# Attention between two feed-forward phases: value matmuls at other steps of a head pair, their eviction on ScalarE, one batch's output by single token tiles

## The chip, the core and the metric

The kernel runs on 1 core of one Trainium2 chip. The metric is the device time of one launch in microseconds (us). The engines are TensorE (PE; its weight loads are a row of their own, PEld), VectorE (DVE), ScalarE (ACT), GpSimd (POOL) and SyncE (SP), which issues the DMAs. PSUM has 8 banks of 512 float32 per partition.

## What is computed

Two batches of 1024 tokens with 128 channels go through a feed-forward block (itself an attention with 16 small heads and a mixture of expert projections), then a causal attention with one shared key/value head of 64, then the feed-forward block again. The middle part is the one that matters here:

```python
q = (x @ Wq).reshape(b, n, 16, 64).transpose(0, 2, 1, 3) * scale
kv = concatenate([null_kv, x @ Wkv], axis=1)        # keys and values are the same
sim = einsum('bhid,bjd->bhij', q, kv)               # causal mask
attn = softmax(sim)
out = einsum('bhij,bjd->bhid', attn, kv)
x = x + out.reshape(b, n, 16 * 64) @ Wout
```

x is the layer-normed input inside the attention; each block adds to the stream.

## The kernel before

The attention goes by head pairs: 8 pairs of 2 heads in each of 2 batches, 16 pairs in all. A pair has 16 steps (`STEPS`): query tiles 0 to 3 of head 0, the same of head 1 (the lower half of the tokens), then query tiles 4 to 7 of either head (the upper half). A step works on 128 queries with 129, 257, ... 1024 keys, so steps 3, 7, 11 and 15 are the longest of their fours.

The steps run through a pipeline with its order written out per engine. In step t TensorE makes the scores of tile t (`a_score_tile`, L1387 and L1389, the mask added by L1394) into one of two pairs of banks, by turns; it waits for the exponential of tile t-2 first. Then come the transposes of tile t-4 (`a_transposes`, L1407; `A_LAG` is 4), in two halves of 64 queries in two banks. DVE reduces the maximum (L1021), copies the second half of the transposes of tile t-4 (L1046) and makes the reciprocal of the sum of tile t-2 (L1040). ACT copies the first half (L727) and makes the exponential of tile t (L720). GpSimd multiplies the probabilities by the reciprocal (L637), ahead of the transposes. Every engine takes its instructions in order.

Into this go, on TensorE:

- the value matmuls `a_values` (L1423), in parts of two key tiles, all into bank 7 (`PV_BANK`). The lower half has two parts, the upper half four. They run in the next pair: lower in its steps 0 and 1 (`V0_STEPS`), upper in its steps 4, 5, 8, 12 (`V1_STEPS`; 4, 5, 8, 9 in the first pair of the second batch). At the end of a half DVE evicts the bank (`o_evac`, L1056)
- the next pair's queries in two halves (`queries`, L1369) in steps 3 and 6, evicted in part by ACT (L705) and in part by DVE (L1015, `query_1`) one step later; then SP copies them across partitions (`build_q_s`)
- in the first pair of the second batch, steps 13 and 14, the output of the first batch (`outputs`, L1433 and L1434): each time four token tiles of nine matmuls, in bank 7, and DVE adds them to x (`add_out`, L1063)

Transposes and queries share three banks (`T_BANKS`), taken by turns in a list of 34 takes a pair (`TAKES`). 34 is not a multiple of 3: the last take of a pair, the second half of the transposes of tile 11 in step 15, is put into a bank by hand, and `taken_before` finds which eviction a take has to wait for. DVE's order in step t is maximum(t), copy(t-4), reciprocal(t-2), eviction of a half of the values, `query_1`, evicted upper half, add. ACT's is copy(t-4), query, exponential(t).

Of the kernel before, what the change touches and what calls it, by code (L numbers as in the profile page):

```python
# [7 lines left out]
ALU = mybir.AluOpType  # L8
# [8 lines left out]
def build(nc, x_in, a_wq, a_wkv, a_null, a_wout, f_wq, f_bq, f_wk, f_bk, f_wv, f_bv,  # L17
# [22 lines left out]
    with ExitStack() as ctx:  # L40
# [157 lines left out]
        ay_done = sem("ay_done")  # L198
        x_loaded = [sem(f"x_loaded_{b}") for b in range(B)]
# [62 lines left out]
        for t in range(NS):  # L262
            TAKES += [("T", (t - A_LAG) % NS, half) for half in range(2)]
            if t in Q_STEPS:
                TAKES.append(("Q", Q_STEPS.index(t), 0))
# [3 lines left out]
        def taken_before(take, pair):  # L269

            i = TAKES.index(take)
            for back in range(1, 2 * len(TAKES)):
                turn, j = pair + (i - back) // len(TAKES), (i - back) % len(TAKES)
                kind, n, half = TAKES[j]
                if TAKE_BANK[TAKES[j]] != TAKE_BANK[take]:
                    continue
                if kind == "T":
                    tile = NS * turn + n - (NS if n >= NS - A_LAG else 0)
                    if tile >= 0:
                        return kind, half, tile  # L280
                elif 0 <= turn < B * PAIRS - 1:
                    return kind, n, turn + 1
            return None
# [368 lines left out]
        def _(act):  # L652
# [46 lines left out]
            def query_0(pg, par, h):  # L699

                if h == 0 and (not isinstance(pg, int) or pg >= 2):
                    act.wait_ge(a_scores, NS * pg - NS)
                act.wait_ge(proj_done, 2 * pg + h + 1)
                bank = TAKE_BANK["Q", h, 0] if pg else (PV_BANK, Q_BANK)[h]
                nc.scalar.activation(q_s[0:AD, par, 0, h * HALF:(h + 1) * HALF], ps[0:AD, bank, :], ACT.Copy,  # L705
                                     scale=A_SCALE).then_inc(q0_ready, 1)
# [16 lines left out]
            def a_evac(pg, t):  # L723
                qh, hh, qt = STEPS[t]
                m = qt + 1
                act.wait_ge(tr_done[0], NS * pg + t + 1)
                nc.scalar.activation(probs_T[qh][:, hh, 0:m, (qt % 4) * P:(qt % 4) * P + ROWS],  # L727
                                     ps[:, TAKE_BANK["T", t, 0], 0:m * ROWS].rearrange("p (k q) -> p k q", q=ROWS), ACT.Copy).then_inc(evac_act, 1)

            def attention():  # L730
# [13 lines left out]
                def body(b, pl, first, last):  # L744
                    for k in range(2):
                        pg = b * PAIRS + pl + k
                        for t in range(NS):
                            if first:
                                second_batch(k, t)
                            if t >= A_LAG:  # L750
                                a_evac(pg, t - A_LAG)
                            elif not (first and k == 0):
                                a_evac(pg - 1, NS + t - A_LAG)
                            if t - 1 in Q_STEPS and not (last and k == 1):
                                query_0(pg + 1, (k + 1) % 2, Q_STEPS.index(t - 1))
                            a_exps(pg, t)
                for b in range(B):
                    body(b, 0, b == 0, False)
                    for i in range(1, PAIRS // 2 - 1):
                        body(b, i * 2, False, False)  # L760
                    body(b, PAIRS - 2, False, b == B - 1)
                for t in range(NS - A_LAG, NS):
                    a_evac(B * PAIRS - 1, t)

                norm_std(2 * B, 0)
                norm_T(2 * B, 0, 5)
# [56 lines left out]
        def _(dve):  # L823
# [185 lines left out]
            def query_1(pg, par, h):  # L1009
# [4 lines left out]
                bank = TAKE_BANK["Q", h, 0] if pg else (PV_BANK, Q_BANK)[h]  # L1014
# [27 lines left out]
            def a_evac(pg, t):  # L1042
# [4 lines left out]
                                      ps[:, TAKE_BANK["T", t, 1], 0:m * ROWS].rearrange("p (k q) -> p k q", q=ROWS)).then_inc(evac_dve, 1)  # L1047
# [6 lines left out]
            def o_evac(pg, pl, qh):  # L1054
                dve.wait_ge(apv_done, 2 * pg + qh + 1)
                nc.vector.tensor_scalar(o_T[:, bass.ds(pl, 1), qh * HALF:(qh + 1) * HALF].rearrange("p a b -> p (a b)"),  # L1056
                                        ps[:, PV_BANK, :], 1.0, None, ALU.mult).then_inc(pv_bank_free, 1)

            def add_out(b, g, bank):

                dve.wait_ge(ay_done, 2 * b + g + 1)
# [3 lines left out]
            def attention():  # L1065
                dve.sem_inc(pv_bank_free, 2)

                def second_batch(pair, t):
# [10 lines left out]
                    if (pair, t) == (1, 15):  # L1079
                        null_scores_in(1, PV_BANK)  # L1080

                def body(b, pl, switch, first, last):
                    for k in range(2):
                        pg = b * PAIRS + pl + k
                        turn = switch and k == 0
                        before = (b - 1, PAIRS - 1) if turn else (b, pl + k - 1)
                        for t in range(NS):
                            if first:
                                second_batch(k, t)
                            a_maximum(pg, t)  # L1090
                            if t >= A_LAG:
                                a_evac(pg, t - A_LAG)
                            elif not (first and k == 0):
                                a_evac(pg - 1, NS + t - A_LAG)
                            if t >= 2:
                                a_recip(pg, t - 2)
                            elif not (first and k == 0):
                                a_recip(pg - 1, NS + t - 2)
                            if t - 1 == V0_STEPS[-1] and not (first and k == 0):
                                o_evac(pg - 1, before[1], 0)  # L1100
                            if t - 1 in Q_STEPS and not (last and k == 1):
                                query_1(pg + 1, (k + 1) % 2, Q_STEPS.index(t - 1))
                            if t - 1 == (V1_TURN if turn else V1_STEPS)[-1] and not (first and k == 0):
                                o_evac(pg - 1, before[1], 1)
                            if turn and t - 1 in Y_STEPS:
                                add_out(b - 1, Y_STEPS.index(t - 1), PV_BANK)
                for b in range(B):
                    body(b, 0, b > 0, b == 0, False)
                    for i in range(1, PAIRS // 2 - 1):
                        body(b, i * 2, False, False, False)  # L1110
                    body(b, PAIRS - 2, False, False, b == B - 1)
                pg = B * PAIRS - 1
                for t in range(NS - 2, NS):
                    a_recip(pg, t)
                o_evac(pg, PAIRS - 1, 0)
                for t in range(NS - A_LAG, NS):
                    a_evac(pg, t)

                norm(2 * B, 0)
                o_evac(pg, PAIRS - 1, 1)  # L1120
# [64 lines left out]
        def _(pe):  # L1185
# [162 lines left out]
            def wait_taken(take, pair):  # L1348

                before = taken_before(take, pair)  # L1350
                if before is not None:
                    kind, n, g = before
                    if kind == "Q":
                        pe.wait_ge(q0_ready, 2 * g + n + 1)
                        pe.wait_ge(q1_ready, 2 * g + n + 1)
                    else:
                        pe.wait_ge(evac_dve if n else evac_act, g + 1)

            def queries(pg, b, h):

                if pg:
                    wait_taken(("Q", h, 0), pg - 1)
                    bank = TAKE_BANK["Q", h, 0]
# [34 lines left out]
            def a_transposes(pg, t):  # L1398
# [3 lines left out]
                for half in range(2):  # L1402
                    wait_taken(("T", t, half), pg + (1 if t >= NS - A_LAG else 0))
                for j in range(qt + 1):
                    for half in range(2):
                        rows = slice(half * ROWS, (half + 1) * ROWS)
                        ins = nc.tensor.transpose(ps[:, TAKE_BANK["T", t, half], j * ROWS:(j + 1) * ROWS],  # L1407
# [4 lines left out]
            def a_values(pg, b, qh, k0, part):  # L1412

                nk = 4 * (qh + 1)
                if part == 0:
                    done = NS * pg + max(s for s in range(NS) if STEPS[s][0] == qh) + 1
                    pe.wait_ge(evac_dve, done)
                    pe.wait_ge(evac_act, done)
                    pe.wait_ge(pv_bank_free, k0)
                for kt in (2 * part, 2 * part + 1):  # L1420
# [188 lines left out]
```

## Time and profile before

| | us |
|---|---|
| three runs, median | 1379.18 |
| lowest, highest | 1374.53, 1388.82 |
| the profiled execution, its own time | 1376.7 |
| its span, first to last instruction | 1375.0 |
| TensorE busy | 1193.7 (87%) |
| VectorE busy | 1078.4 (78%) |
| ScalarE busy | 926.4 (67%) |
| mean granted TensorE clock | 0.955 |

The attention's scores run from 402 to 963 us of the span. Busy times are shares of an engine's time in which an instruction of it runs; idle time in the rows below stands in brackets or behind a bar with the instruction that ended it.

### The profile page before, as it was taken

What the parts mean: (1) busy time and instruction counts of PE and PEld (TensorE: products, weight loads), DVE (VectorE), ACT (ScalarE), POOL (GpSimd) and SP (SyncE); (2) the same over time, 40 slices, a digit from 0 to 9 for tenths busy, and PEclk for the clock granted to TensorE, in tenths of its full rate; (3) what the DMA queues carried; (4) which work ended last, traced back from release to release, by engine and by line L of the source; (5) the groups of instructions that cost most, each with busy time, mean ns of one, the idle gap of its engine ahead of it and who ended that gap; (6) DMA issues with size and microseconds to landing.
All of it is one profiled execution on the core that took longest, in us unless ns stands there. A gap on an engine that the chain in (4) does not pass through costs nothing. (4 is left out here: it accounts for less than half of the span.)

```text
span 1375.0 us, 32035 instructions
## 1 busy us (share of the span) xinstructions
PE 1193.7 (87%) x10916; PEld 513.0 (37%) x10916; DVE 1078.4 (78%) x1813; ACT 926.4 (67%) x1969; POOL 304.2 (22%) x534
## 2 busy tenths in 40 slices
PE   4499999999978888888888888888868999999996
PEld 3122222222245545444465444445542222222222
DVE  6899999999886666666645666666569999999997
ACT  3189999988945656555534565556325999998894
POOL 4300000022103333333312333334222000000100
PEclk9689999999989999999999999999978999999998
DMA  4711212452110000000000000000043222236422
GB/s 111 220 45 52 56 53 68 93 89 71 40 31 17 17 16 17 16 17 16 16 17 17 16 17 17 17 16 2 1 138 105 64 52 55 62 76 98 75 55 62
DMA packets 51792, 69.54 MB, mean 51 GB/s; under 512 B 21168, under 2 KB 29296, under 8 KB 51696
## 3 DMA queue, kind: packets, MB, share of 16 engines
q1 hardware_dynamic: 51696, 68.26, 20.4%
q8 instruction: 60, 0.98, 0.3%
q14 instruction: 36, 0.29, 0.1%
HBM read 37.30 MB, written 22.54 MB: 44 GB/s over the span
## 5 line engine op out<-in xcount | busy, mean ns | idle before, releaser
L949 DVE TENSOR_REDUCE neg_max<-ps 128x1 f32<-128x1024 f32 x512 | 591.8, 1217 | 26.1 <-PE ps L1243 24.3
L785 ACT ACTIVATE arena<-ps 128x512 f32<-128x512 f32 x1024 | 545.4, 597 | 86.1 <-PE ps L1258 73.9
L1021 DVE TENSOR_REDUCE a_neg_max<-ps 128x1 f32<-128x129 f32 (+7 forms) x256 | 192.7, 753 | 196.9 <-PE ps L1394 196.4
L1258 PE MATMUL ps<-arena 50*128 50x512 bf16 x1024 | 323.6, 388 | 17.1 <-ACT arena L785 9.9
L1274 PE MATMUL ps<-arena 128*32 128x256 f32 (+1 forms) x3584 | 316.2, 425 | 8.6 <-ACT arena L785 3.1
L1243 PE MATMUL ps<-arena 48*128 48x512 bf16 x1024 | 296.9, 396 | 15.9 <-DVE neg_max L949 14.8
L637 POOL TENSOR_SCALAR arena<-arena,a_rsum 128x128 f32<-128x128 f32 (+7 forms) x256 | 192.1, 750 | 405.8 <-DVE a_rsum L1040 405.5
L727 ACT ACTIVATE arena<-ps 128x64 f32<-128x64 f32 (+7 forms) x256 | 104.5, 408 | 193.4 <-PE ps L1407 191.0
L1387 PE MATMUL ps<-arena 64*128 64x321 f32 (+7 forms) x512 | 191.4, 454 | 33.1 <-ACT arena L720 29.9
L720 ACT ACTIVATE arena<-ps,a_neg_max 128x129 f32<-128x129 f32 (+7 forms) x256 | 189.1, 739 | 40.1 <-DVE a_neg_max L1021 34.7
L1389 PE MATMUL ps<-arena 64*128 64x128 f32 (+6 forms) x512 | 195.2, 462 | 0.0
L1258 PEld LDWEIGHTS ps<-arena 50*128 50x128 bf16 x1024 | 74.0, 94 | 297.2 <-ACT arena L785 267.5
L1407 PE MATMUL ps<-ident,arena 64*128 64x64 f32 x2304 | 137.5, 229 | 46.5 <-DVE arena L1046 26.1
L1423 PE MATMUL ps<-arena 128*64 128x512 f32 (+3 forms) x768 | 155.3, 530 | 0.8 <-DVE arena L1046 0.8
L1407 PEld LDWEIGHTS ps<-ident,arena 64*128 64x128 f32 x2304 | 124.8, 140 | 81.4 <-issue 51.4
L1274 PEld LDWEIGHTS ps<-arena 128*32 128x32 f32 x3584 | 71.2, 108 | 165.6 <-issue 91.9
L545 POOL CAST max_parts<-neg_max 128x8 bf16<-128x8 f32 x64 | 12.2, 191 | 511.2 <-DVE neg_max L949 511.2
L1046 DVE COPY arena<-ps 128x64 f32<-128x64 f32 (+7 forms) x256 | 115.2, 450 | 9.7 <-PE ps L1407 9.7
L1387 PEld LDWEIGHTS ps<-arena 64*128 64x128 f32 x512 | 77.2, 189 | 116.5 <-ACT arena L720 59.7
L1389 PEld LDWEIGHTS ps<-arena 64*128 64x128 f32 x512 | 77.4, 189 | 0.0
L1243 PEld LDWEIGHTS ps<-arena 48*128 48x128 bf16 x1024 | 57.8, 94 | 36.2 <-DVE neg_max L949 26.4
L1423 PEld LDWEIGHTS ps<-arena 128*64 128x64 f32 x768 | 49.1, 142 | 55.8 <-issue 43.9
(125 smaller groups left out, 832.3 us busy)
## 6 DMA issues: line engine op xcount, KB each, us to landing
arena<-stack_dram SPq DMA_DIRECT2D x128, 192.0 KB, 3.4
stack_dram<-arena SPq DMA_DIRECT2D x48, 256.0 KB, 3.8
o_dram<-arena SPq DMA_DIRECT2D x32, 256.0 KB, 2.1
arena<-arena SPq DMA_DIRECT2D x32, 256.0 KB, 3.7
arena<-o_dram SPq DMA_DIRECT2D x30, 256.0 KB, 4.3
arena<-max_dram SPq DMA_DIRECT2D x256, 1.0 KB
x<-in_L_attn_x SPq DMA_DIRECT2D x2, 512.0 KB, 5.2
max_dram<-max_T SPq DMA_DIRECT2D x64, 8.0 KB, 1.6
```

Of the source, the lines that this page charges most:

```text
L637: nc.gpsimd.tensor_scalar(a_probs[:, t % RING, 1:n], a_probs[:, t % RING, 1:n], a_rsum[:, t:t + 1], 1.0, ALU.mult, ALU.mult).then_inc(a_no ...
L720: nc.scalar.activation(a_probs[:, t % RING, c0:c0 + a_keys(t)], a_region(t), ACT.Exp, bias=a_neg_max[:, t:t + 1], accum_out=a_sum[:, t:t + ...
L785: nc.scalar.activation(probs[:, t, :], ps[:, EXP_BANK[t], :], ACT.Exp, scale=F_SCALE).then_inc(probs_ready, 1)
L949: nc.vector.tensor_reduce(neg_max[:, g, t:t + 1], ps[:, bank:bank + 2, :].rearrange("p a b -> p (a b)"), AX, ALU.max, negate=True).then_in ...
L1021: ins = nc.vector.tensor_reduce(a_neg_max[:, t:t + 1], a_region(t), AX, ALU.max, negate=True)
L1243: ins = nc.tensor.matmul(ps[:, bank + h, :], stack[rows, g, 0, t * P:(t + 1) * P], stack[rows, g, 1, h * HALF:(h + 1) * HALF], start=True, ...
L1258: ins = nc.tensor.matmul(ps[:, bank, :], stack[rows, g, 1, kt * P:(kt + 1) * P], stack[rows, g, 0, h * HALF:(h + 1) * HALF], start=True, s ...
L1274: ins = nc.tensor.matmul(ps[row:row + 32, PV_BANK, cols], v_unit[:, g, t // 2, :], probs[:, t, cols], start=j == 0 and c0 == 0 and g % 2 == 0,
L1387: nc.tensor.matmul(ps[:, mid, HALF - split + head:HALF], q_s[0:AD, par, hh, cols], k_f[0:AD, b, k0 + head:k0 + split], start=True, stop=True)
L1389: nc.tensor.matmul(ps[:, mid + 1, 0:n - split], q_s[AD:P, par, hh, cols], k_f[AD:P, b, k0 + split:k0 + n], start=True, stop=False)
L1407: ins = nc.tensor.transpose(ps[:, TAKE_BANK["T", t, half], j * ROWS:(j + 1) * ROWS], a_probs[rows, t % RING, 1 + j * P:1 + (j + 1) * P], i ...
L1423: ins = nc.tensor.matmul(ps[hh * AD:(hh + 1) * AD, PV_BANK, q0:HALF], av[:, b, kt, :], probs_T[qh][:, hh, kt, q0:HALF], start=kt == 0, sto ...
```

## The change

- Lower half's values: steps 15 and 0 (16) instead of 0 and 1 of the next pair. Upper half's: steps 5, 9, 11, 13 of the next pair (21, 25, 27, 29), in the second batch's first pair too. `o_evac` is an ACT copy at the head of the step after the last part.
- The second query half moves from step 6 to step 7.
- `TAKES` is one list over all 16 pairs; each take waits for the one three places before it, with no place set by hand.
- The first batch's output comes as eight single token tiles, in steps 8, 10, 12, 14 of pair 8 and 2, 8, 10, 12 of pair 9, in banks of the rotation; DVE adds each, at the end of its next step.
- DVE's order in a step is now `query_1`, reciprocal(t-2), maximum(t), copy(t-4), add; ACT's is `o_evac`, query, copy(t-4), exponential(t).
- At the end of the attention the last lower half is in steps 15 and 16, and the last upper half is evicted by ACT after its `norm_std`. The null scores of the second batch come in step 3 of pair 1 (before, step 14).

The core of the diff:

```diff
-        V0_STEPS = (0, 1)
-        Q_STEPS = (3, 6)
-        V1_STEPS = (4, 5, 8, 12)
-        V1_TURN = (4, 5, 8, 9)
-        Y_STEPS = (13, 14)
+        N_PAIRS = B * PAIRS
+        V_STEPS = ((15, 16), (21, 25, 27, 29))
+        Q_STEPS = (3, 7)
+        Y_STEPS = [NS * PAIRS + k for k in (8, 10, 12, 14)] + [NS * PAIRS + NS + k for k in (2, 8, 10, 12)]
+        LAST_STEP = NS * (N_PAIRS - 1) + V_STEPS[1][-1]
...
-        TAKE_BANK = {k: T_BANKS[i % 3] for i, k in enumerate(TAKES)}
-        TAKE_BANK[TAKES[-1]] = next(b for b in T_BANKS if b not in (TAKE_BANK[TAKES[-2]], TAKE_BANK[TAKES[0]]))
...
+        for s in range(LAST_STEP + 1):
+            if 0 <= s - A_LAG < NS * N_PAIRS:
+                TAKES += [("T", s - A_LAG, half) for half in range(2)]
+            if query_half(s):
+                TAKES.append(("Q", *query_half(s)))
+            if s in Y_STEPS:
+                TAKES.append(("Y", Y_STEPS.index(s), 0))
+        TAKE_BANK = {take: T_BANKS[i % 3] for i, take in enumerate(TAKES)}
+        TAKEN_BEFORE = {take: TAKES[i - 3] if i >= 3 else None for i, take in enumerate(TAKES)}
...
# ScalarE
+            def o_evac(pg, qh):
+
+                act.wait_ge(apv_done, 2 * pg + qh + 1)
+                nc.scalar.activation(o_T[:, pg % PAIRS, qh * HALF:(qh + 1) * HALF], ps[:, PV_BANK, :], ACT.Copy).then_inc(pv_bank_free, 1)
...
+                for s in range(LAST_STEP + 2):
+                    pg, t = divmod(s, NS)
+                    second_batch(pg, t)
+                    for qh in range(2):
+                        part = value_part(s - 1, qh)
+                        if part and part[1] == len(V_STEPS[qh]) - 1 and s <= LAST_STEP:
+                            o_evac(part[0], qh)
+                    if s and query_half(s - 1):
+                        query_0(query_half(s - 1)[0], query_half(s - 1)[0] % 2, query_half(s - 1)[1])
+                    if 0 <= s - A_LAG < NS * N_PAIRS:
+                        a_evac(*divmod(s - A_LAG, NS))
+                    if pg < N_PAIRS:
+                        a_exps(pg, t)
...
# VectorE
-            def o_evac(pg, pl, qh):
-                dve.wait_ge(apv_done, 2 * pg + qh + 1)
-                nc.vector.tensor_scalar(o_T[:, bass.ds(pl, 1), qh * HALF:(qh + 1) * HALF].rearrange("p a b -> p (a b)"),
-                                        ps[:, PV_BANK, :], 1.0, None, ALU.mult).then_inc(pv_bank_free, 1)
+            def add_token_tile(k):
+
+                dve.wait_ge(ay_done, k + 1)
+                ins = nc.vector.tensor_tensor(x[:, k, :], ps[:, TAKE_BANK["Y", k, 0], 0:C], x[:, k, :], ALU.add)
+                ins.then_inc(x_ready if k % 4 == 3 else y_added, 1)
...
+                for s in range(LAST_STEP + 1):
+                    pg, t = divmod(s, NS)
+                    second_batch(pg, t)
+                    if s and query_half(s - 1):
+                        query_1(query_half(s - 1)[0], query_half(s - 1)[0] % 2, query_half(s - 1)[1])
+                    if 0 <= s - 2 < NS * N_PAIRS:
+                        a_recip(*divmod(s - 2, NS))
+                    if pg < N_PAIRS:
+                        a_maximum(pg, t)
+                    if 0 <= s - A_LAG < NS * N_PAIRS:
+                        a_evac(*divmod(s - A_LAG, NS))
+                    if s - 1 in Y_STEPS:
+                        add_token_tile(Y_STEPS.index(s - 1))
...
# TensorE
+            def token_tile_out(k):
+
+                pe.wait_ge(pv_bank_free, 2 * PAIRS - 1 + k // 4)
+                wait_taken(("Y", k, 0))
+                bank, tok = TAKE_BANK["Y", k, 0], slice(k * P, (k + 1) * P)
+                for p in range(PAIRS):
+                    nc.tensor.matmul(ps[:, bank, 0:C], o_T[:, p, tok], wout[:, p, :], start=p == 0, stop=False)
+                nc.tensor.matmul(ps[:, bank, 0:C], ones[:, :], null_out[:, :], start=False, stop=True).then_inc(ay_done, 1)
```

TensorE's order in a step is as before: scores, transposes, values, queries, then a token tile.

## Rows read from the trace of the kernel before

**Rows 1.** The page, part 1: busy us (share of the span) and instructions

```profile
PE 1193.7 (87%) x10916; PEld 513.0 (37%) x10916; DVE 1078.4 (78%) x1813; ACT 926.4 (67%) x1969; POOL 304.2 (22%) x534
```

**Rows 2.** The page, part 5: busy, mean ns | idle before, releaser

```profile
L1387 PE MATMUL ps<-arena 64*128 64x321 f32 (+7 forms) x512 | 191.4, 454 | 33.1 <-ACT arena L720 29.9
```

**Rows 3.** Busy time by stretch; a pair from its first score to the next pair's

```profile
core 0: us, PE busy (x) PEld busy (x) DVE busy (x) ACT busy (x) POOL busy (x), PEclk, DMA share, GB/s
437.78:673.74 235.96, 201.82 (x2051) 116.57 (x2047) 153.78 (x394) 140.46 (x364) 84.01 (x113) 0.98 0.07 17
673.74:762.23 88.49, 77.00 (x732) 51.06 (x729) 45.02 (x115) 40.14 (x104) 23.99 (x33) 0.98 0.05 13
762.23:933.17 170.94, 146.84 (x1464) 83.89 (x1461) 109.34 (x281) 100.41 (x260) 60.05 (x81) 0.96 0.07 17
933.17:961.47 28.30, 24.22 (x270) 14.70 (x266) 17.93 (x51) 17.50 (x48) 10.56 (x16) 1.00 0.01 2
537.24:570.15 32.91, 28.09 (x296) 16.39 (x293) 21.86 (x57) 20.03 (x52) 11.99 (x17) 1.00 0.07 17
570.15:604.70 34.55, 29.73 (x296) 17.02 (x293) 21.90 (x57) 20.04 (x52) 12.01 (x17) 0.95 0.06 16
553.47:570.15 16.68, 12.82 (x143) 7.80 (x140) 12.86 (x29) 11.12 (x26) 6.09 (x8) 1.00 0.13 32
540.74:548.33 7.59, 7.46 (x88) 4.54 (x86) 5.39 (x15) 4.44 (x13) 2.94 (x5) 1.00 0.02 4
```

**Rows 4.** Timeline of PE in steps 8 to 13: start, us, instruction [idle before <-releaser]

```profile
555.56 0.28 PE L1407 MATMUL ps<-ident,arena 64*128 64x64 f32 x2 [1.19 <-DVE arena L1015]
555.76 1.72 PE L1423 MATMUL ps<-arena 128*64 128x512 f32 x8
557.42 0.59 PE L1387 MATMUL ps<-arena 64*128 64x385 f32 x1
...
560.47 0.69 PE L1387 MATMUL ps<-arena 64*128 64x512 f32 x1 [0.85 <-ACT arena L720]
...
564.59 0.59 PE L1387 MATMUL ps<-arena 64*128 64x385 f32 x1 [0.75 <-ACT arena L720]
```

**Rows 5.** Timeline of DVE in step 8

```profile
554.61 0.69 DVE L1015 TENSOR_SCALAR arena<-ps 64x512 f32<-64x512 f32 x1
```

**Rows 6.** Timeline of PE in step 15 and the next step 0

```profile
567.64 0.69 PE L1387 MATMUL ps<-arena 64*128 64x512 f32 x1 [0.35 <-ACT arena L720]
...
569.56 0.71 PE L1407 MATMUL ps<-ident,arena 64*128 64x64 f32 x16 [0.73 <-DVE arena L1046]
...
571.54 0.53 PE L1407 MATMUL ps<-ident,arena 64*128 64x64 f32 x10 [0.84 <-DVE arena L1046]
572.00 2.93 PE L1423 MATMUL ps<-arena 128*64 128x512 f32 x8
```

**Rows 7.** Timeline of DVE in the same stretch

```profile
568.79 0.62 DVE L1046 COPY arena<-ps 128x448 f32<-128x448 f32 x1
...
570.71 0.68 DVE L1046 COPY arena<-ps 128x512 f32<-128x512 f32 x1
```

**Rows 8.** Evictions of 128x512, by line: duration ns min/median/max, first and last start us

```profile
L1056 DVE TENSOR_SCALAR arena<-ps x32: 671/673/692, 445.3 to 979.1; 128x512 f32<-128x512 f32 x32
L775 ACT ACTIVATE arena<-ps x32: 597/597/598, 92.0 to 1358.9; 128x512 f32<-128x512 f32 x32
```

**Rows 9.** Groups by shape in the quiet pair (537.24 to 570.15), as in rows 2

```profile
L720 ACT ACTIVATE arena<-ps,a_neg_max 128x257 f32<-128x257 f32 x2 | 0.9, 474 | 0.1
L727 ACT ACTIVATE arena<-ps 128x384 f32<-128x384 f32 x2 | 1.0, 492 | 2.0 <-PE ps L1407 2.0
L705 ACT ACTIVATE arena<-ps 64x512 f32<-64x512 f32 x2 | 1.2, 577 | 0.0
```

**Rows 10.** Timeline of PE in the two bursts of output

```profile
706.97 2.05 PE L1433 MATMUL ps<-wout,arena 128*128 128x128 f32 x16
...
717.61 1.16 PE L1433 MATMUL ps<-wout,arena 128*128 128x128 f32 x8 [1.91 <-DVE x L1063]
```

More of the change, by code:

```diff
@@ L198, in build @@
         ay_done = sem("ay_done")
+        y_added = sem("y_added")
         x_loaded = [sem(f"x_loaded_{b}") for b in range(B)]
@@ L269, in taken_before @@
[L269 to L283, printed above, removed]
+        N_PAIRS = B * PAIRS
@@ L703, in query_0 @@
                 act.wait_ge(proj_done, 2 * pg + h + 1)
-                bank = TAKE_BANK["Q", h, 0] if pg else (PV_BANK, Q_BANK)[h]
+                bank = TAKE_BANK["Q", pg, h] if pg else (PV_BANK, Q_BANK)[h]
                 nc.scalar.activation(q_s[0:AD, par, 0, h * HALF:(h + 1) * HALF], ps[0:AD, bank, :], ACT.Copy,
@@ L742, in second_batch @@
                         norm_T_half(B + 1, 1, (t - 7) // 2, PV_BANK)
[L744 to L763, printed above, removed]
+                for s in range(LAST_STEP + 2):
[11 more added lines that the diff above has]
+                        a_exps(pg, t)
                 norm_std(2 * B, 0)
+                o_evac(N_PAIRS - 1, 1)
                 norm_T(2 * B, 0, 5)
@@ L1078, in second_batch @@
                         null_scores_in(0, Q_BANK)
-                    if (pair, t) == (1, 15):
+                    if (pair, t) == (1, 4):
                         null_scores_in(1, PV_BANK)
[L1082 to L1106, printed above, removed]
@@ L1402, in a_transposes @@
                 for half in range(2):
-                    wait_taken(("T", t, half), pg + (1 if t >= NS - A_LAG else 0))
+                    wait_taken(("T", NS * pg + t, half))
                 for j in range(qt + 1):
@@ L1511, in attention @@
-                for part in range(4):
-                    a_values(pg, B - 1, 1, 2 * pg + 3, part)
+                for s in range(LAST_STEP + 1):
+                    pg, t = divmod(s, NS)
+                    if pg == 0:
+                        second_batch(t)
+                    if pg < N_PAIRS:
+                        if pg == PAIRS and t == 0:
+                            pe.wait_ge(keys_ready, B)
+                        a_score_tile(pg, pg // PAIRS, pg % 2, t)
+                    if 0 <= s - A_LAG < NS * N_PAIRS:
+                        a_transposes(*divmod(s - A_LAG, NS))
+                    for qh in range(2):
+                        if value_part(s, qh):
+                            a_values(value_part(s, qh)[0], qh, value_part(s, qh)[1])
+                    if query_half(s):
+                        queries(query_half(s)[0], query_half(s)[0] // PAIRS, query_half(s)[1])
+                    if s in Y_STEPS:
+                        token_tile_out(Y_STEPS.index(s))
+                    if s == NS + 3:
+                        pe.wait_ge(pv_bank_free, 1)
+                        null_scores(1, PV_BANK)
```

125 lines of the change are left out of this document (36 added, 89 removed).

## The prediction

> **What bounds the kernel now.** I read the page first. TensorE (PE) is busy for 87% of the span, VectorE (DVE) 78%, ScalarE (ACT) 67% [rows 1]. That is a mean over two feed-forward phases and the attention between them, and the change touches the attention alone, so I cut that stage by head pair. A pair begins where the first score matmul (L1387) of its step 0 starts. Pairs 1 to 7 take 235.96 us, pairs 8 and 9 (with the first batch's output inside) 88.49, pairs 10 to 14 170.94, and pair 15 up to its step 15 28.30 [rows 3]. A quiet pair, pair 4 (counted from 0), takes 32.91 us and PE works in 28.09 of it; the next one takes 34.55 with 29.73 of work: same instructions, lower granted clock (0.95 for 1.00). In the quiet pair DVE works 21.9 us, ACT 20.0, GpSimd 12.0 [rows 3]. So PE is the nearest bound, and 4.82 us of each pair (15%) are waits of PE. Steps 8 to 15 lose 3.86 of it (16.68 - 12.82), steps 0 to 7 the other 0.96 [rows 3].
>
> The timeline of PE says what each wait is for. In the heavy steps three waits stand in front of scores, each for the exponential of two steps before: 0.85 us in step 11, 0.75 in step 13 [rows 4], 0.35 in step 15 [rows 6]; on the page they are most of the 29.9 us that L1387 waits for ACT [rows 2]. They are a loop: score(t), maximum on DVE, exponential on ACT, then score(t+2) in the same banks. 1.19 us in step 8 is the transpose's wait for a bank that holds the second query half; DVE gets to it (L1015, 554.61, 0.69 us) behind a copy and a reciprocal [rows 4, 5]. 0.73 in step 15 and 0.84 in the next step 0 are transposes waiting for DVE copies (568.79 + 0.62 and 570.71 + 0.68) [rows 6, 7]. The code says why: 34 bank takes a pair do not divide by 3, so the last take is put by hand into the bank of the take just two before it, and both T11 (the transposes of tile 11) and T12 wait for a copy hardly begun. With 0.13 in step 3 the list is 0.35 + 0.85 + 0.75 + 1.19 + 0.73 + 0.84 + 0.13 = 4.84, against 4.82 measured: nothing is unexplained.
>
> The last thing to see is the row at 572.00: the eight value records of step 0 take 2.93 us, while the same eight in the quiet pair's step 8 (also 512 and 384 columns) take 1.72 [rows 4, 6]. The granted clock was at its lower level (1.2 GHz instead of 2.4) right after the waits of 0.73 and 0.84. Seven of the pairs above are 1.5 to 1.7 us longer for it.
>
> **The change part by part.** PE's work is the same. The values are worth, per part, about 1.87 us where both key tiles have all 512 columns, 1.66 for 512 + 384, 0.80 to 0.87 for 256 + 128 (start of the part to start of the next score, as 555.76 to 557.42 [rows 4]). They move from steps 0, 1 (lower) and 4, 5, 8, 12 (upper) to steps 15, 0 and 5, 9, 11, 13.
>
> *Bank rotation.* Now every take waits for the third before it, across pairs too. T11 needs the DVE copy of tile 9 and ACT's of tile 10, T12 needs DVE's of 10 and ACT's of 11, all over before the transposes are due. 0.73 and 0.84 go, minus 1.57 a pair.
>
> *Second query half at step 7.* It is followed by T4 in other banks; T5 in step 9 needs it, 1.1 + 0.65 us of PE work after the query's end. DVE takes it first in its step now: 0.70 and 0.2 of release. Minus 1.19. SP's copy of the queries starts a step later; the pair's first score, which needs it, is eight steps on, half a pair, so nothing.
>
> *Fill of the heavy steps.* The loop score(9) to score(11) is 3.05 us (557.42 to 560.47), and PE had 2.2 of work in it, the rest is its wait [rows 4]. With 1.87 of values in step 9 it has 4.07. Step 11 to 13: loop 4.12 (560.47 to 564.59), work 3.37 with the 0.87 of values in step 12, now 3.37 - 0.87 + 1.66 = 4.16. Step 13 to 15: loop 3.05 (564.59 to 567.64), work 2.70, now 2.70 + 0.80 = 3.50 [rows 4, 6]. Steps 14, 15 and 0 get 1.66 and 0.80 over loops of 3.4 and 4.1. Minus 0.85, 0.75, 0.35.
>
> *What the light steps lose.* Steps 1 to 4 took 7.59 us with 0.80 and 1.87 of values in them [rows 3]; without these and a wait of 0.13 PE has 4.8 of work there: 0.81, 0.86, 2.5 with the query half, 0.57. ACT starts step 1 with the new eviction: DVE's took 0.673 us, and ACT copies the same 128x512 out of PSUM elsewhere in 0.597 [rows 8]. From the start of step 1: eviction to 0.65, copy of tile 13 (0.49) from 0.85 to 1.34, exponential of step 1 (0.47, with what follows it 0.57) to 1.91 [rows 9]; score(3) can start at 1.96, where PE comes at 1.67. Plus 0.3. Copy of 14 to 2.44, exponential of step 2 to 3.11, T15 and the first query half to 4.46 on PE: no wait. Then the copy of 15, the exponential of step 3 to 4.82, the query half on ACT (0.577 [rows 9]) to 5.40, copy of tile 0 to 5.62. T1 in step 5 needs that bank: 5.77, PE comes at 5.58. Plus 0.2, and the 1.87 of values behind it lets ACT and DVE catch up. The second query half needs DVE's copy of tile 2, behind a reduction of 0.56: plus 0.2. Behind each of these waits stand the next scores in PE's queue; the sums contain that. DVE loses 2 x 0.67 and does its reciprocal ahead of the maximum, so GpSimd's normalization starts no later; its 12 us stay hidden four steps ahead. The upper half's eviction comes in ACT's step 14 behind the exponential of 13 and is done about 1.3 us before the values of step 15 want the bank. Cost: nothing; without that cover up to 0.6.
>
> New pair: 28.1 + 0.3 + 0.2 + 0.2 = 28.8 us. From below it is bounded by PE's work, 28.1; from above I take both ACT evictions in full and one loop wait back (1.2 + 0.85), 30.8. I take 28.8, since the same way of adding gives the old pair to 0.02.
>
> *Output.* A token tile costs 2.05 + 0.35 = 2.40 us of PE [rows 10], eight are 19.2, whether in two bursts or apart. The 1.91 us in which the second burst waits for the add of the first goes [rows 10]. One single tile (step 2 of pair 9) is added behind the copy of tile 15, and the query half behind it waits some 1.2. Eight adds of 128 columns replace two of 512, on a DVE with 7 us to spare a pair.
>
> *Clock.* With PE's waits down to 0.7 us, spread over light steps, I take no low stretch in the pairs; the 1.6 us of each is in the old lengths. Of the pages, "TensorE: Matmul & The Clock Gate" of the Trainium skill (A second HAM failure mode) speaks against this: a kernel that cycles through PSUM banks idles a little between groups and so keeps falling to the lower clock. Rotation over three banks stays here; the trace agrees that short waits go before the low stretches. By that rule the time would be the first rival's.
>
> **The sum.** Pairs 1 to 7: 235.96 - 7 x 28.8 = 34.4. Pairs 8 and 9: 88.49 - (57.6 + 19.2 + 1.2) = 10.5. Pairs 10 to 14: 170.94 - 144.0 = 26.9. Pair 15 to its step 15: 28.8 less step 15 (3.5), less what the missing queries free (0.8 + 1.1) = 23.4, so 4.9. Pair 0 gets 1.66 of values into its step 15 and loses the 0.73: -1. Tail: the last T12 to T15 wait for normalization, with the lower values hidden there before; now these waits are open, so nothing is won. Together 75.7 us. The profiled run took 1376.7 (span 1375.0), so 1301.0; the median of the three runs is 2.5 above it. Prediction 1303 us.
>
> **The rivals.** *The low clock stays* (0.12): seven falls, 1.6 each, 11 us, 1314. For it: the output burst's fall came after only 1.3 us of waiting. Against: all others follow two waits that go. *ACT and DVE bound the light steps* (0.17): a pair of 30.3, 15 x 1.5 = 22 more, 1325. For it: in steps 0 to 3 ACT has 5.1 us of work and has to wait for PE in between, and PE 5.9. *The heavy steps stay bound by DVE* (0.06): DVE works 12.86 of their 16.68 us, and with the values between, each maximum starts later; only banks and query pay, 2.76 x 15 = 41, so about 1338. *Other side* (0.03): bank 7 is now released by ACT, in order behind exponentials, and PE stands in front of its next scores until then. If the eviction slips by a whole step of ACT (3.5 us) at both halves, a pair takes 35.8 and the kernel 1303 + 15 x 7 = 1408. It decides from a slip of 2.5 us a half on (the mean old pair is 33.8); the cover is 1.3 in step 15, four steps in step 1 to 5. *The order of the single output tiles gives back what the pairs win* (0.02): 20 us or more of it.
>
> **The numbers.** The forecast has 0.60 and by itself spans 1290 to 1316. With the clock and the light steps 0.89 are covered by 1288 to 1334, where the upper bound of the pair (30.8) lies. A measurement of this kernel can tell about 1% from no change; faster by more than that has 0.95, within it 0.02, slower 0.03.
>
> **What would show it.** Pairs of 28.5 to 29.5 us with PE busy for 97% or more; no idle time of L1407 before L1046 or L1015 in steps 8, 15 and 0; L1387 waiting for ACT only in step 3, under 0.5 us; the value groups of step 0 at about 0.8 us; the steps with a token tile longer by its 2.4 us and nothing else. A step 3 of over 4 us would show ACT as the new bound; granted clock under 0.98 in pairs 1 to 7 would be the clock rival; waits of L1423 for ACT's eviction the last one.

## The result and the profile after

| | before | after |
|---|---|---|
| median us (runs) | 1378.43 (4) | 1289.26 (4) |
| lowest to highest | 1374.53 to 1388.82 | 1287.49 to 1291.22 |
| profiled execution, its span | 1376.7, 1375.0 | 1291.22, 1289.5 |

The ratio is 0.9342, 95% interval 0.929 to 0.9395: 89 us faster, where 76 were forecast. 1289 lies at the very bottom of the wide range (1288 to 1334) and just below the 1290 to 1316 that the forecast by itself spanned. The direction and the place of the gain were right; the new pair of heads was costed 0.8 us too long.

The page after (parts 1 and 5), beside [rows 1, 2]. L1363 and L1365 are the scores now, L1370 their mask, L1383 the transposes, L1404 the values:

```profile
PE 1173.5 (91%) x10916; PEld 508.9 (39%) x10916; DVE 1063.0 (82%) x1787; ACT 941.8 (73%) x2001; POOL 304.1 (24%) x534
...
L1363 PE MATMUL ps<-arena 64*128 64x321 f32 (+7 forms) x512 | 188.3, 451 | 4.7 <-DVE neg_s_null L1052 1.9
```

Scores waited 33.1 us before and wait 4.7 now; the 29.9 us behind ACT's exponentials are gone. DVE and ACT do about the same work in a span shorter by 85.5 us.

The same stretches as in [rows 3], each again from a pair's first score: pairs 1 to 7; 8 and 9; 10 to 14; 15 up to its step 15; and a quiet pair (3). Columns: stretch and its length, busy time of each engine, granted clock, DMA:

```profile
442.56:639.20 196.64, 192.78 (x2049) 115.61 (x2047) 146.06 (x380) 146.71 (x379) 84.00 (x112) 1.00 0.08 20
639.20:715.94 76.74, 74.87 (x731) 49.75 (x729) 43.97 (x117) 42.75 (x109) 24.00 (x32) 1.00 0.06 15
715.94:856.11 140.17, 137.61 (x1463) 82.32 (x1461) 104.13 (x271) 104.81 (x271) 60.01 (x80) 1.00 0.08 20
856.11:879.86 23.75, 22.42 (x259) 14.11 (x259) 16.23 (x48) 17.30 (x47) 10.82 (x15) 1.00 0.01 2
498.92:526.91 27.99, 27.51 (x294) 16.45 (x293) 20.82 (x55) 20.93 (x55) 11.99 (x16) 1.00 0.08 20
```

| stretch | before | after | won | forecast |
|---|---|---|---|---|
| pairs 1 to 7 | 235.96 | 196.64 | 39.3 | 34.4 |
| pairs 8, 9 with the output | 88.49 | 76.74 | 11.8 | 10.5 |
| pairs 10 to 14 | 170.94 | 140.17 | 30.8 | 26.9 |
| pair 15 up to step 15 | 28.30 | 23.75 | 4.6 | 4.9 |
| the rest | 851.3 | 852.2 | -0.9 | -1 |

The quiet pair is 27.99 us with PE busy for 27.51: 0.48 of wait (4.82 before). The granted clock is 1.00 in all of them, where it was 0.96 to 0.98. The last line is the remainder of the span (1375.0 and 1289.5) and holds pair 0, the end of the attention and both feed-forward phases.

### The profile page after: what moved, and what is told of

Same layout as the page of the kernel before. It is cut to its first block and busy times, and to the rows that moved or that the text cites. A ratio compares the mean times of both kernels' runs of the same rounds, so it can differ in the third digit from the quotient of the medians.

```text
span 1289.5 us, 32074 instructions
## 1 busy us (share of the span) xinstructions
PE 1173.5 (91%) x10916; PEld 508.9 (39%) x10916; DVE 1063.0 (82%) x1787; ACT 941.8 (73%) x2001; POOL 304.1 (24%) x534
## 5 line engine op out<-in xcount | busy, mean ns | idle before, releaser
L949 DVE TENSOR_REDUCE neg_max<-ps 128x1 f32<-128x1024 f32 x512 | 591.3, 1215 | 28.3 <-PE ps L1218 26.3
L1021 DVE TENSOR_REDUCE a_neg_max<-ps 128x1 f32<-128x129 f32 (+7 forms) x256 | 191.8, 749 | 115.3 <-PE ps L1370 114.3
L1365 PE MATMUL ps<-arena 64*128 64x128 f32 (+6 forms) x512 | 192.9, 458 | 0.0
L1363 PE MATMUL ps<-arena 64*128 64x321 f32 (+7 forms) x512 | 188.3, 451 | 4.7 <-DVE neg_s_null L1052 1.9
L1383 PE MATMUL ps<-ident,arena 64*128 64x64 f32 x2304 | 140.6, 228 | 9.7 <-DVE arena L1046 4.5
L1383 PEld LDWEIGHTS ps<-ident,arena 64*128 64x128 f32 x2304 | 129.3, 139 | 42.5 <-issue 26.9
L1404 PE MATMUL ps<-arena 128*64 128x512 f32 (+3 forms) x768 | 144.4, 498 | 1.3 <-DVE arena L1046 0.8
L1363 PEld LDWEIGHTS ps<-arena 64*128 64x128 f32 x512 | 77.5, 190 | 81.8 <-issue 52.1
L1365 PEld LDWEIGHTS ps<-arena 64*128 64x128 f32 x512 | 78.6, 192 | 0.0
L1404 PEld LDWEIGHTS ps<-arena 128*64 128x64 f32 x768 | 47.0, 136 | 50.3 <-issue 38.6
```

Source lines behind the costliest of these rows:

```text
L949: nc.vector.tensor_reduce(neg_max[:, g, t:t + 1], ps[:, bank:bank + 2, :].rearrange("p a b -> p (a b)"), AX, ALU.max, negate=True).then_in ...
L1021: ins = nc.vector.tensor_reduce(a_neg_max[:, t:t + 1], a_region(t), AX, ALU.max, negate=True)
L1363: nc.tensor.matmul(ps[:, mid, HALF - split + head:HALF], q_s[0:AD, par, hh, cols], k_f[0:AD, b, k0 + head:k0 + split], start=True, stop=True)
L1365: nc.tensor.matmul(ps[:, mid + 1, 0:n - split], q_s[AD:P, par, hh, cols], k_f[AD:P, b, k0 + split:k0 + n], start=True, stop=False)
L1383: ins = nc.tensor.transpose(ps[:, TAKE_BANK["T", NS * pg + t, half], j * ROWS:(j + 1) * ROWS], a_probs[rows, t % RING, 1 + j * P:1 + (j + ...
L1404: ins = nc.tensor.matmul(ps[hh * AD:(hh + 1) * AD, PV_BANK, q0:HALF], av[:, pg // PAIRS, kt, :], probs_T[qh][:, hh, kt, q0:HALF], start=kt ...
```

## The experiments

Each kernel was timed in three rounds beside the kernel before. All are read by one instrument as well, the quiet pair of the profiled execution: its length, and PE's busy time in it. The median of the kernel before was 1379.1, 1381.1 and 1380.2 us beside the three groups.

### First group: the changed kernel with one part undone

**Old bank rule** (`u_bank`).

```diff
-        TAKE_BANK = {take: T_BANKS[i % 3] for i, take in enumerate(TAKES)}
-        TAKEN_BEFORE = {take: TAKES[i - 3] if i >= 3 else None for i, take in enumerate(TAKES)}
...
+            if i and OF_STEP[take] // NS != OF_STEP[TAKES[i - 1]] // NS:
+                place = 0
+                if TAKE_BANK[TAKES[i - 1]] == T_BANKS[0]:
+                    TAKE_BANK[TAKES[i - 1]] = next(b for b in T_BANKS if b not in (TAKE_BANK[TAKES[i - 2]], T_BANKS[0]))
+            TAKE_BANK[take] = T_BANKS[place % 3]
...
```

A take then waits for the last earlier take of its own bank.

> The changed kernel with the old rule for banks alone: rotation starts anew with each pair, and the last take (second half of T11, step 15) goes by hand into the bank of the take two before it. Theory 'cover' (what a wait costs depends on the work now around it): T12's wait of 0.84 us is hidden by the 1.7 us of values that now stand between T11 and T12; T11's wait for the copy of tile 10 is left, about 0.5 us a pair, so 8 us over the changed kernel, about 1297. Rival 'each part by itself' (the waits of the kernel before come back whole): 1.57 us a pair and some stretches at the low clock, 24 to 34 us, 1313 to 1323.

Measured: 1293.08 us (1292.35 to 1294.46), 4 more than the changed kernel; the pair is 28.55. On PE's timeline the one wait that came is T11's:

```profile
548.89 0.71 PE L1394 MATMUL ps<-ident,arena 64*128 64x64 f32 x16 [0.37 <-DVE arena L1057]
```

"Cover" holds: of 0.73 + 0.84 [rows 6] only 0.37 is left. The 4 us understate it. In the profiled executions pairs 1 to 14 take 419.95 us here and 413.55 in the changed kernel, 6.4 more, while the feed-forward phase ahead of the attention, which the edit does not touch, happened to be 5.2 shorter (the first score stands at 400.09 and at 405.30). So a few us of a median are scatter from outside the attention, and the pairs are the sharper reading.

**Second query half at step 6** (`u_query`): `Q_STEPS = (3, 6)`.

> The changed kernel with the second query half at step 6 again. Theory 'cover': DVE takes the query first in its step now, 0.95 us after the matmul the bank is free and T4 comes 1.7 us after it, so no wait: within 2 us of the changed kernel. Rival 'the step does it': the wait of 1.19 us in front of T4 comes back, 15 times, 18 us, about 1307.

Measured: 1305.58 us (1302.34 to 1307.89), 16 more; pair 28.92. That is the rival's number, but not its mechanism. PE's timeline at the start of step 9:

```profile
538.69 0.59 PE L1363 MATMUL ps<-arena 64*128 64x385 f32 x1 [0.76 <-ACT arena L721]
```

No transpose waits for long for the query's bank, as "cover" had said; instead the score of step 9 waits 0.76 us for the exponential of step 7. With the query in step 6, steps 7 and 8 hold only 0.78 and 1.1 us of PE work, and the loop from score 7 to score 9 takes 2.6. The query at step 7 is filler for that loop. "Cover" had the wrong time, the rival the wrong reason.

**Values at their old steps** (`u_values`): `V_STEPS = ((16, 17), (20, 21, 24, 28))`, and the last token tile in step 11.

> The changed kernel with the values at their old steps (0 and 1; 4, 5, 8, 12), the last token tile one step earlier than before so that the upper half of pair 8 does not overwrite it. Theory 'cover': the waits of scores for exponentials in steps 11, 13, 15 come back (1.95 us a pair) and one or two more, since steps 9 to 15 are again bound by the loop over DVE and ACT: pair of 30.5 to 31 us, some falls of the clock, 38 to 50 us over the changed kernel, 1327 to 1339. Rival 'banks and query do it': 0 to 10 us over it, with the values' place worth little.

Measured: 1325.86 us (1323.48 to 1327.07), 37 more, just under the 38 to 50 of "cover"; pair 30.17. The three waits of scores are back to within 0.01, beside [rows 4, 6] (the third is the 0.34 of step 15):

```profile
580.30 0.69 PE L1363 MATMUL ps<-arena 64*128 64x512 f32 x1 [0.85 <-ACT arena L721]
...
584.42 0.59 PE L1363 MATMUL ps<-arena 64*128 64x385 f32 x1 [0.75 <-ACT arena L721]
```

**Evictions on DVE** (`u_evict`): the two `o_evac` as a DVE copy at the head of the same steps.

> The changed kernel with both evictions of the values on DVE, at the head of the same steps. Theory 'cover': DVE has 7 us of idle time a pair and the loops over it are shorter than PE's work now, so 0 to 5 us over the changed kernel. Rival 'DVE's load did it': 2 x 0.67 us a pair come back in full, 20 us, about 1309.

Measured: 1290.67 us (1286.37 to 1295.23); pair 27.99, the changed kernel's to the hundredth. DVE is busy for 21.86 us of the pair instead of 20.82, ACT for 19.96 instead of 20.93. Which engine evicts the values is worth nothing that can be measured, as long as it does so at the head of the step.

### Second group: DVE's order, and one part alone

The base `a_none` has everything undone that the first group undid and DVE's order as well; only the single token tiles are left (and ACT's order of query and copy, and the place of the second batch's null scores). DVE evicts the values behind its reciprocal again. `a_rotation`, `a_values` and, in the third group, `a_order` add one part to it; `a_order` moves this eviction too, to the head of DVE's step.

**DVE's order** (`u_order`), the rest as changed; the lines taken out stood ahead of the maximum and the copy, the new ones stand behind them:

```diff
-                    if s and query_half(s - 1):
-                        query_1(query_half(s - 1)[0], query_half(s - 1)[0] % 2, query_half(s - 1)[1])
-                    if 0 <= s - 2 < NS * N_PAIRS:
-                        a_recip(*divmod(s - 2, NS))
...
+                    if 0 <= s - 2 < NS * N_PAIRS:
+                        a_recip(*divmod(s - 2, NS))
+                    if s and query_half(s - 1):
+                        query_1(query_half(s - 1)[0], query_half(s - 1)[0] % 2, query_half(s - 1)[1])
```

> The changed kernel with DVE's order of before: maximum(t), copy(t-4), reciprocal(t-2), query. Theory 'cover': in step 8 the second query half now comes behind maximum, copy and reciprocal, free about 3.1 us after its matmul, while T5 wants the bank after 1.75: a wait of 1.2 to 1.4 us in step 9, and about 0.6 in step 5 by the first half, 15 times: 1307 to 1319. Rival 'order is neutral' (the place of the queries and of the values is what counts): within 3 us of the changed kernel.

Measured: 1333.96 us (1330.36 to 1336.07), 45 more: the largest of all, and over the 1307 to 1319 of "cover"; pair 30.60. PE's timeline over one pair, in steps 3, 5 and 9:

```profile
535.21 0.71 PE L1383 MATMUL ps<-ident,arena 64*128 64x64 f32 x16 [0.42 <-POOL arena L638]
...
538.97 0.34 PE L1383 MATMUL ps<-ident,arena 64*128 64x64 f32 x4 [1.09 <-POOL arena L638]
...
546.80 0.34 PE L1383 MATMUL ps<-ident,arena 64*128 64x64 f32 x4 [1.20 <-POOL arena L638]
```

The view names GpSimd's normalization each time, because it was the last semaphore to change before the transposes started. For 1.09 and 1.20 that is not the cause. T1 in step 5 needs the normalization of tile 1 (256 columns), and that was long done; what ended at 538.78 was tile 2's. T1 also needs the bank of the first query half, and DVE was copying that out until 538.71:

```profile
536.95 0.48 POOL L638 TENSOR_SCALAR arena<-arena,a_rsum 128x256 f32<-128x256 f32 x1 [0.73 <-DVE a_rsum L1040]
...
538.02 0.69 DVE L1015 TENSOR_SCALAR arena<-ps 64x512 f32<-64x512 f32 x1
```

From the end of L1015 to the transpose it is 0.26 us here, 0.26 in step 9 (545.85 + 0.69 to 546.80), and 0.26 in the kernel before, where the view names L1015 itself (554.61 + 0.69 to 555.56 [rows 4, 5]). So both are waits for the query halves, which DVE takes last, as "cover" had expected with 0.6 and 1.2 to 1.4. Only the 0.42 of step 3 is a normalization: tile 15's ended at 535.16, and its reciprocal had stood behind a copy. The pair is 2.6 us longer: 1.20 in step 9, 0.94 more in step 5, 0.27 more in step 3 and 0.2 of busy time.

**Everything undone but the single tiles** (`a_none`).

> The kernel before rebuilt on the changed one: old bank rule, queries at 3 and 6, values at their old steps, DVE evicts and has its old order; only the single token tiles are left (and ACT's order within a step: query, copy, exponential). Theory: single tiles save the add's wait of 1.9 us and a fall of the clock of 1.6, so 3 to 5 us below the kernel before, about 1375. Rival: the bursts starved DVE and ACT for 24 us and cost more than PE's time, 8 us or more below, 1370 or less.

Measured: 1376.83 us (10 runs, 1372.19 to 1383.78), ratio to the kernel before 0.9978 (0.9956 to 1.0001): at most the 3 to 5 us of the theory, and not clear of nothing. So the single tiles, ACT's order and the null scores together are worth no more than that at the old places. The quiet pair is 32.92 with PE busy for 28.10, the old pair again ([rows 3]: 32.91, 28.09).

**Rotation alone** (`a_rotation`).

> As the rebuilt kernel before (single token tiles, all else old), with the unbroken rotation of banks alone. Theory 'each wait is its own': T11's 0.73 and T12's 0.84 go in 15 pairs and with them the falls of the clock behind them (11 us): 1338 to 1345. Rival 'the wait moves on': with no values in steps 13 to 15 the loop over DVE and ACT sets these steps, the score of step 15 or 1 waits instead: 5 to 12 us won, about 1365.

Measured: 1350.56 us (1347.33 to 1355.98), 26 below `a_none`; pair 32.01. Between the two theories: T12's 0.84 is gone, T11's 0.73 has moved on, to the first score of the next pair, which now waits for the exponential of step 14:

```profile
597.13 0.24 PE L1368 MATMUL ps<-arena 64*128 64x1 f32 x1 [0.78 <-ACT arena L721]
```

0.91 x 15 is 14 us; the other 12 I put down to the clock (below).

**Values alone** (`a_values`).

> As the rebuilt kernel before, with the values alone at their new steps (15, 0; 5, 9, 11, 13). Theory: 0.85 + 0.75 + 0.35 go in each pair, T12's 0.84 lies behind the values of step 15, the falls of the clock go; T11's 0.73 and the query's 1.19 stay: 2.8 x 15 = 42 and 11 us below 1375, 1322 to 1333. Rival 'DVE still bounds the heavy steps': 1350 or more.

Measured: 1334.62 us (1329.93 to 1339.48), 42 below `a_none`; pair 31.03. The scores wait no more; the transposes do:

```profile
569.47 0.71 PE L1399 MATMUL ps<-ident,arena 64*128 64x64 f32 x16 [0.42 <-POOL arena L649]
...
573.23 0.34 PE L1399 MATMUL ps<-ident,arena 64*128 64x64 f32 x4 [1.09 <-POOL arena L649]
...
580.08 0.28 PE L1399 MATMUL ps<-ident,arena 64*128 64x64 f32 x2 [1.19 <-DVE arena L1021]
```

0.42 and 1.09 are the waits of `u_order`, here without any other new part: the first for tile 15's normalization, the second for the first query half (L1021 is `query_1` here and ended at 572.97, 0.26 before the transpose). The values left step 4, where they had hidden it; DVE's order takes both away. 1.19 is the second query half's, as before, and of T11's 0.73 there is 0.37 left.

### Third group: order alone, and three attempts at a better kernel

> As the rebuilt kernel before (single token tiles, the last one a step earlier; all else old), with DVE's new order alone: query, reciprocal, maximum, copy. Theory 'the order pays only with the values moved' (its worth in the changed kernel, 45 us, is a wait of T1 and T5 for normalizations that hardly exists at the old places): the wait of 1.19 us in step 8 goes, the rest stays, 18 us below 1377, about 1359. Rival 'the order is the main cause by itself': 30 us or more below, 1347 or less.

Measured for `a_order`: 1337.43 us (1336.76 to 1338.45), 39 below `a_none`; pair 31.08. That is the rival's number. The three waits of scores stay (0.85, 0.74, 0.35); on PE's timeline T12's is the one that changed:

```profile
533.46 0.52 PE L1399 MATMUL ps<-ident,arena 64*128 64x64 f32 x10 [1.12 <-DVE arena L1052]
```

The query's 1.19 and T11's 0.73 of [rows 4, 6] are gone, T12's grew from 0.84 to 1.12: 1.64 us of waits, 1.84 of pair length, 28 us in fifteen pairs, and I put the rest down to the clock. But this kernel does not test the order alone. The 1.19 goes because DVE takes the query first. The 0.73 goes with the eviction of the values, which moved to the head of the step; before and in `a_order`:

```profile
567.21 0.67 DVE L1056 TENSOR_SCALAR arena<-ps 128x512 f32<-128x512 f32 x1
...
558.06 0.68 DVE L1062 TENSOR_SCALAR arena<-ps 128x512 f32<-128x512 f32 x1
```

Before, it stood in front of the maximum of step 14 and put off the copy that T11 waits for: that copy ended 1.77 us after the start of score 15 (569.41, 567.64), in `a_order` 0.97 after it (562.12, 561.15). Earlier in the step the eviction falls into time in which DVE waited for PE (0.89 us before the maximum of step 13, in the kernel before). That the reciprocal's new place has a part in this gain, no run shows.

**One token tile in step 5 instead of 2** (`i_y`), `Y_STEPS` with `(5, 8, 10, 12)`.

> The changed kernel with one token tile moved from step 2 to step 5 of pair 9. That tile's add stands behind the copy of tile 15, and the first query half behind it waits about 0.8 us in step 3; both theories: 1 us below the changed kernel, 1288; if nothing, the step-5 place costs as much.

Measured: 1290.53 us (1290.01 to 1290.72), not to be told from the changed kernel. In the trace pair 9 is 38.33 us instead of 38.77, 0.44 won: the wait of 1.06 for the tile's add is gone, and one of 0.40 stands in front of the transposes of step 7.

**The second part of the lower values in step 2** (`i_v18`), `V_STEPS = ((15, 18), ...)`.

> As i_y, with the lower half's second part of values in step 2 instead of 0, between T14 and T15. Theory: what is left of PE's waits (0.18 in step 2, 0.15 in step 3, 0.15 in step 5) is transposes waiting for a copy just begun; the part covers the one in step 3, 0.15 x 15 = 2 us less, 1286. Rival: steps 0 and 1 then have 2.3 us of PE work in which exponentials 14 to 0 are not done in time: a new wait of 0.5 us or more in step 1 or 2, 5 us or more slower.

Measured: 1291.24 us (1290.94 to 1292.37); pair 28.09 instead of 28.00. The wait in step 3 is gone, 0.09 stands in step 0, and nothing is won.

**First query half in step 2** (`i_q2`), `Q_STEPS = (2, 7)`.

> As i_y, with the first query half in step 2 instead of 3. Theory: it covers T15's wait and takes the queries' release out of step 5: 0.3 x 15 = 4 us less, 1284. Rival: step 3 then has only its scores and transposes in front of step 4, so score 4 or 5 waits for the exponential: the same sum or slower, 1288 to 1296.

Measured: 1295.3 us (1293.07 to 1297.46); pair 28.48. Step 4 is 1.63 us instead of 0.33, 0.39 and 0.37 of it (the latter at its end) waits: the rival's reason and number. None of the three is better than the changed kernel; with 0.48 of wait in 28.0 there is little left to win by moving work between steps.

## Why the prediction was right or wrong

**What bounds the kernel.** Right. The list of seven waits was complete, and the large ones were found again where what removes them was left out: 0.85, 0.75 and 0.34 in `u_values`, T12's 0.84 as 1.12 in `a_order`, 0.73 (moved on as 0.78) in `a_rotation`, 1.19 in `a_rotation` and `a_values`, and as 1.20 in `u_order`. Two of them go by other means than the text has: 0.73 without the new bank rule, when DVE evicts the values earlier (`a_order`), and 1.19 by DVE's order alone, with the query still in step 6 (`a_order`, `u_query`).

**"From below it is bounded by PE's work, 28.1".** This is the step that failed. The pair takes 28.0 with 0.48 of wait in it, so PE's busy time went down to 27.5 with the same instructions: 28.1 was not the work, but the work and something that comes with each wait. The quiet pairs, from the windows view (length, PE busy; the next column is the number of waits of 0.12 us or more on PE's timeline in that pair):

| kernel | pair us | PE busy | waits |
|---|---|---|---|
| a_none, as before | 32.92 | 28.10 | 7 |
| a_rotation | 32.01 | 27.98 | 6 |
| u_values | 30.17 | 27.94 | 5 |
| a_order | 31.08 | 27.89 | 5 |
| a_values | 31.03 | 27.79 | 5 |
| u_order | 30.60 | 27.71 | 4 |
| u_bank | 28.55 | 27.70 | 4 |
| u_query | 28.92 | 27.68 | 4 |
| changed | 27.99 | 27.51 | 3 |

`a_none` in the windows view (the changed kernel's row stands above):

```profile
474.69:507.61 32.92, 28.10 (x297) 16.39 (x293) 21.87 (x57) 20.23 (x52) 11.95 (x17) 1.00 0.07 17
```

Busy time falls with the number of waits, by about 0.59 / 4 = 0.15 us for each one less, more or less alike whatever its length. Four more kernels with three waits (those of 0.09 and 0.10 counted) do not fall out of line: 27.52 in `i_y`, 27.54 in `i_q2`, 27.56 in `u_evict`, 27.65 in `i_v18`. So a tenth of a us is scatter with the order of the work.

The timelines show where it comes from. In an unbroken run the next group starts while the record of the group before is still open; ahead of a wait nothing covers its end. The same two mask matmuls, first in the changed kernel (step 1), then in the kernel before, ahead of the 1.19 of [rows 4]:

```profile
500.87 0.22 PE L1370 MATMUL ps<-mask_m,mask_w 64*128 64x64 bf16 x2
500.92 0.51 PE L1383 MATMUL ps<-ident,arena 64*128 64x64 f32 x10
...
554.16 0.22 PE L1394 MATMUL ps<-mask_m,mask_w 64*128 64x64 bf16 x2
```

Above, transposes start 0.05 us after the mask matmuls, so 0.17 of the 0.22 is counted once for both. Below, all of 0.22 counts, and the next start is at 555.56. The size fits the 0.15, but no run isolates it, and the ends of matmuls are modelled in the profile. For a sum it means: PE's busy time is no floor while it still has waits in it.

**The sum.** Of the 0.8 us that a quiet pair is shorter than forecast, 0.6 are PE's busy time and 0.2 the waits of the light steps. The profiled execution was forecast at 1301.0 and took 1291.2: the 9.8 us are the lines of the table, 4.9 + 1.3 + 3.9 - 0.3. The other 4 us between 1303 and 1289 are no mechanism. I had added 2.5 because the median before lay that much above the profiled execution; after the change it lies 2.0 below.

**Light steps.** I had 0.3 + 0.2 + 0.2 in steps 3, 5 and 7; the trace has them like this:

```profile
502.11 0.65 PE L1383 MATMUL ps<-ident,arena 64*128 64x64 f32 x14 [0.18 <-DVE arena L1046]
```

0.18 in step 2, about 0.15 in 3 and in 5, none in 7. In steps 2 and 3 they are transposes waiting for a copy of the tile before. In step 5 it is T1 waiting for the bank of the first query half, as the text had it, though by DVE's copy (505.33 + 0.69, then 0.26 to 506.27 as above) and not by ACT's. The score of step 3 never waits for ACT. ACT's eviction was costed as if it held that score; with the eviction on DVE the pair is as long (`u_evict`).

**Bank rotation, minus 1.57.** The waits went, but the price belongs to no single part. Undone it costs 0.56 a pair, alone it brings 0.91 of pair length.

**Second query half, minus 1.19.** Right that the wait goes and that DVE's taking it first is enough; wrong that step 7 has nothing more in it: the filler for scores 7 to 9 is worth 0.92 a pair (`u_query`). The place in DVE's order is worth more: without it 1.09 and 1.20 stand in steps 5 and 9 (`u_order`). The text priced the second half alone; the first half's wait had been hidden by the values of step 4, which the change takes away.

**Fill of the heavy steps.** Right, mechanism and size: 2.18 a pair undone, for 1.95 of waits.

**"DVE ... does its reciprocal ahead of the maximum, so GpSimd's normalization starts no later".** True, and its price is small as far as the runs show: undone, tile 15's normalization holds PE for 0.42 us in step 3, where 0.15 of another wait stands now. No run moves the reciprocal by itself. The 2.6 us a pair of DVE's whole order are mostly the query halves.

**Output.** 76.74 against 78.0. A single tile costs 2.5 us, not 2.40 (pair 8 has four and is 9.98 longer than a quiet pair); the query's wait behind the tile in step 2 is 1.06 where 1.2 was forecast. Moving the tile wins 0.44 of it.

**Clock.** Right that no fall (a stretch at the lower level) is left in the pairs. The window 437.78 to 673.74 before had 0.98 [rows 3], the one after has 1.00. The price is better known now: every part alone ends the falls but for one (in `a_order`, pair 1, granted clock 0.95), and that is why the parts do not add. Parts alone bring 26, 42 and 39 us, and in each 12 to 14 us are left over when fifteen times what its quiet pair won is taken off (26.3 - 13.7, 42.2 - 28.4, 39.4 - 27.6). That this remainder is the clock is my reading; the size fits, since the profiled execution of `a_none` had nine falls of 1.6 us each.

**The rule of the pages.** "TensorE: Matmul & The Clock Gate" of the Trainium skill (A second HAM failure mode) says that in a kernel that cycled through PSUM banks TensorE idled a little between groups, often enough to fall to the lower clock again and again. Here three banks are cycled before and after. In `a_rotation`, with six waits and 4.0 us of idle time in every pair, the granted clock is 1.00 over 450 us of pairs:

```profile
470.00:920.00 450.00, 393.38 (x4048) 235.24 (x4050) 291.23 (x758) 268.97 (x696) 160.20 (x215) 1.00 0.07 17
```

So the cycling itself does not do it here. The long pairs went with the place where 0.73 and 0.84 stood with 1.1 us of work between them, but that place is not enough for a fall: the pairs at 537.24 and 570.15 have the same waits, and only in the second did the clock fall [rows 3]. Nor does the idle time of a pair decide: pair 9 of `a_rotation` has 6.95 us of waits in 44.91 and the clock at 1.00, pair 1 of `a_order` 3.95 in 33.15 and 0.95. What sets off a fall stays open. The rival that I drew from the page did not come true.

**The other rivals.** ACT as the bound of the light steps: no, 20.9 us busy in 28.0, and no score there waits for it. DVE as the bound of the heavy ones: no; even with DVE's old order the values' move takes all three waits of scores away (`a_values`), and what it leaves are the query halves, a normalization and T11. The slower side: no value matmul waits for ACT's eviction, and `u_evict` puts its engine at nothing.

## What to carry to other kernels

Where TensorE waits in short pieces, list them with their releaser until the list gives the stretch's idle time; then put independent matmuls into those steps in which the loop over the other engines is longer than TensorE's work, and check the light steps that they leave. With each such move ask which waits the moved work had hidden. On the other engines, an instruction that frees a bank for TensorE (here the copy of a query half, 0.69 us) must stand ahead of those that themselves wait for TensorE. The releaser that a view names is the last semaphore to change, which need not be the one that was missing: compare it with the tile that the waiting instruction needs, and with the delay from a release to a start elsewhere. Parts of such a change don't add, so a part's price needs both runs, alone and undone.

## What the runs showed of the hardware that was not expected

A wait of TensorE costs more than the idle time that the profile shows, some 0.15 us of busy time in these pairs (28.10 with seven waits, 27.51 with three, same instructions): the end of the last record before it is covered by nothing. And the falls of the clock do not follow the total of idle time: in the kernel before, pairs with the same 4.82 us of waits took 32.9 us or 34.5, the longer ones with a granted clock of 0.95; in `a_rotation`, where one wait of 0.78 stands for the 0.73 and the 0.84, none was.
